# Expert layers of a two-block network: transposes spread over the chunk, sums per eight tiles, gates in 15 steps

## What is computed

```python
def _ffn(x, router_w, router_b, expert_w, expert_b):      # 8 experts, 64 channels
    router_probs = softmax(x @ router_w + router_b)
    top_p, top_i = top_k(router_probs, 2)
    top_p = top_p / sum(top_p)
    expert_out = einsum('bnd,edc->bnec', x, expert_w) + expert_b
    gathered = take_along_axis(expert_out, top_i[..., None], axis=2)
    return einsum('bnk,bnkc->bnc', top_p, gathered)

t = t + _ffn(_ln_t(t), ...)      # _ln_t: layer norm over the 64 channels
```

## Time and profile before

| | |
|---|---|
| median of three runs | 1204.75 us |
| the profiled execution | 1205.99 us, span of its instructions 1204.2 us |
| layer 1, first gate product to last | 276.1 to 585.7 us |
| layer 2, first gate product to last | 888.3 to 1191.6 us |
| busy: PE, DVE, POOL, ACT | 912.3, 911.8, 660.4, 576.0 us |
| granted TensorE clock, mean | 0.886 of 2.4 GHz |

### The profile page before, as it was taken

How to read it: one execution, slowest core, us unless ns; L and a number is a source line. 1 busy time by engine, 2 the same in 40 slices (tenths; PEclk the granted TensorE clock), 3 DMA queues, 4 the chain that set the end, 5 groups by cost and what they waited for, 6 DMA issues and landing times.

```text
span 1204.2 us, 24945 instructions
## 1 busy us (share of the span) xinstructions
PE 912.3 (76%) x8490; PEld 699.6 (58%) x8490; DVE 911.8 (76%) x2088; ACT 576.0 (48%) x1163; POOL 660.4 (55%) x532
## 2 busy tenths in 40 slices
PE   5964469776778777887369999999247887788887
PEld 5863468663445444554269999999124454445454
DVE  6978976677977788799956777754568788777884
ACT  1336854476655565530034444442576556555500
POOL 1542000325877687778474443310437777787787
PEclk9955579977889999999879999999559998899998
DMA  9865600010899992000358778883000000000000
GB/s 387 280 280 118 165 2 1 2 43 0 325 397 398 396 397 90 1 2 1 116 169 281 266 253 277 268 268 118 1 1 18 36 19 35 17 24 29 36 32 39
DMA packets 52865, 168.18 MB, mean 140 GB/s; under 512 B 13616, under 2 KB 13872, under 8 KB 51120
## 3 DMA queue, kind: packets, MB, share of 16 engines
q1 hardware_dynamic: 52784, 167.18, 39.3%
HBM read 98.68 MB, written 68.49 MB: 139 GB/s over the span
## 4 chain that ended last, share of the span: by engine, by line
PE 40%; DVE 24%; ACT 17%; issue 9%; POOL 6%; DMA 2%; ACTq 1%; DVEq 0%; SPq 0%; POOLq 0%
PE pair L1364 19%; ACT pair L1047 10%; DVE R L784 5%; PE pair L1332 5%; PE pair L1282 3%; PE pair L1329 3%; POOL R L458 3%; DVE R L829 3%; DVE work L612 2%; PE pair L1318 2%; PE pair L1319 2%; DVE R L721 2%; PE pair L1296 2%; DVE work L603 2%; ACT X L1081 1%
## 5 line engine op out<-in xcount | busy, mean ns | idle before, releaser
L784 DVE TENSOR_TENSOR R<-pair,R 128x1024 f32<-128x1024 f32 x256 | 310.0, 1215 | 96.7 <-PE pair L1319 90.6
L458 POOL TENSOR_TENSOR R<-R 128x1024 f32<-128x1024 f32 x128 | 304.4, 2378 | 123.1 <-DVE R L784 122.0
L1364 PE MATMUL pair<-R 128*128 (+4 forms) x2880 | 227.8, 243 | 21.6 <-DVE R L836 21.6
L1364 PEld LDWEIGHTS pair<-R 128*128 128x128 f16 x2880 | 224.9, 98 | 24.7 <-issue 22.0
L1318 PE MATMUL pair<-work,R 128*128 128x512 f16 x512 | 203.3, 397 | 35.6 <-DVE R L784 35.5
L1319 PE MATMUL pair<-work,R 128*128 128x512 f16 x512 | 201.2, 393 | 0.0
L1047 ACT ACTIVATE pair<-X,work 128x64 f32 (+1 forms) x496 | 168.8, 394 | 25.2 <-DVE R L721 20.0
L468 POOL TENSOR_TENSOR R<-R 128x512 f32<-128x512 f32 x128 | 163.1, 1274 | 11.3 <-POOL R L458 2.5
L845 DVE COPY R<-R 128x1152 f32<-128x1152 f32 x64 | 91.4, 1429 | 78.9 <-PE pair L1364 78.1
L1329 PE MATMUL pair<-X,ident_sb 128*128 128x256 f32 (+1 forms) x256 | 89.6, 434 | 76.3 <-ACT X L1081 67.0
L1332 PE MATMUL pair<-R,ident_sb 128*128 128x256 f32 x512 | 145.2, 410 | 0.0
(11 more groups left out here) (131 smaller groups left out, 1408.4 us busy)
## 6 DMA issues: line engine op xcount, KB each, us to landing
taps_halves<-R SPq DMA_DIRECT2D x128, 458.5 KB, 6.4
R<-taps_halves SPq DMA_DIRECT2D x64, 917.0 KB, 4.7
R<-spec_re SPq DMA_DIRECT2D x34, 256.0 KB, 4.1
X<-x_rows SPq DMA_DIRECT2D x4, 2048.0 KB, 20.9
R<-x_chan SPq DMA_DIRECT2D x4, 2048.0 KB, 25.3
X<-x_tok SPq DMA_DIRECT2D x4, 2048.0 KB, 13.9
out<-X SPq DMA_DIRECT2D x16, 512.0 KB, 2.6
R<-taps SPq DMA_DIRECT2D x2, 603.0 KB, 7.2
```

What stands on the lines that cost most here:

```text
L458: pool.tensor_tensor(h, pr[:, :, 0:256], pr[:, :, 256:512], ALU.add).then_inc(half_ready, 1)
L784: dve.tensor_tensor(pr.rearrange("p (k c) -> p k c", c=C), pair[p % 2][:, :].rearrange("p (k c) -> p k c", c=C), g.unsqueeze(2).to_broadca ...
L1364: mm = pe.matmul(acc[:, y0:y1, x0:x1, :], blocks[i % 2][:, ks, 2 - y, 1 - x, :], src[:, y0 + y:y1 + y, x0 + x:x1 + x, :], start=(ks == 0 a ...
```

## The change

All of it is in the expert layers.

1. **Sums per eight tiles.** `sum_quad` becomes `sum_octet`: six matmuls in one go, four times a chunk, ahead of pairs 3, 7, 11 and 15 (SUM_AT = 3), for the octet of the four pairs that end four pairs earlier. ACT copies 512 columns instead of 256, at pairs 0, 4, 8, 12. There are eight buffers for POOL's results instead of four.
2. **Transposes spread.** TURN_AT goes from (0, 1, 3, 5) to (9, 13, 1, 5), the first two of them in the chunk before; the routing matmuls follow (ROUTE_AT). `copy_parts` waits for fewer pairs.
3. **Halves of normalisation.** The eight ACTIVATEs are issued as four and four, in two neighbouring pairs, with `copy_parts` between them.
4. **Gates in 15 steps** over pairs 8 to 14. The two small TENSOR_SCALARs (L762, L766) go; ACT computes one of them (`scale_c`), the other is folded away.
5. **One function table.** A set of functions with ln and exp is loaded once at the start.
6. PARTS_AT shifts two of the statistics by a pair.

```diff
-        quarter = [R1[:, 12288 + 512 * i:12288 + 512 * (i + 1)] for i in range(4)]
+        quarter = [R1[:, 512 * i:512 * (i + 1)] for i in (24, 25, 26, 27, 0, 1, 2, 3)]
...
-        GATE_STEPS = 17
+        GATE_STEPS = 15
...
-        NORM_AT, LOW_AT, TURN_AT, ROUTE_AT = (5, 9, 13, 1), (8, 12, 0, 4), (0, 1, 3, 5), (1, 2, 4, 6)
-        NORM_AHEAD, LOW_AHEAD = 3, 2
-        SUM_LAG, COPY_AT = 3, 0
-        GATES_AT = {7: (0, 1), 8: (2, 3), 9: (4, 5), 10: (6, 7), 11: (8, 9), 12: (10,), 13: (11, 12, 13, 14), 14: (15, 16)}
-        PARTS_AT = (0, 1, 1, 2, 3, 3, 5, 6)
+        NORM_AT, LOW_AT, TURN_AT, ROUTE_AT = (5, 9, 13, 1), (8, 12, 0, 4), (9, 13, 1, 5), (0, 1, 3, 7)
+        FIRST_ROUTE = (2, 3, 4, 7)
+        NORM_AHEAD, LOW_AHEAD, TURN_AHEAD = 3, 2, 2
+        SUM_AT, SUM_LAG, COPY_LAG = 3, 1, 2
+        GATES_AT = {8: (0, 1), 9: (2, 3), 10: (4, 5), 11: (6, 7), 12: (8, 9), 13: (10, 11), 14: (12, 13, 14)}
+        PARTS_AT = (1, 2, 2, 3, 3, 5, 6, 7)
...
                 elif i == 11:
-                    dve.wait_ge(exped, n + 1)
-                    ins = dve.tensor_scalar(den, gs[6], SCALE, SCALE, ALU.mult, ALU.add)
+                    ins = dve.scalar_tensor_tensor(out=scratch, in0=scratch, scalar=-5e29, in1=other, op0=ALU.is_le,
+                                                   op1=ALU.subtract)
                 elif i == 12:
+                    dve.wait_ge(exped, 2 * n + 2)
                     ins = dve.reciprocal(first_share, den)
                 elif i == 13:
-                    ins = dve.tensor_scalar(second_share, first_share, -1.0, 1.0 / SCALE, ALU.mult, ALU.add)
-                elif i == 14:
-                    ins = dve.scalar_tensor_tensor(out=e(first), in0=e(scratch), scalar=-5e29, in1=over_e(first_share),
-                                                   op0=ALU.is_le, op1=ALU.mult)
-                elif i == 15:
-                    ins = dve.tensor_tensor(e(logits), e(logits), over_e(second_share), ALU.mult)
+                    ins = dve.tensor_tensor(e(scratch), e(scratch), over_e(first_share), ALU.mult)
                 else:
-                    ins = dve.tensor_tensor(gate[q], logits, first, ALU.add)
+                    ins = dve.scalar_tensor_tensor(out=gate[q], in0=other, scalar=1.0 / SCALE, in1=scratch, op0=ALU.mult,
+                                                   op1=ALU.add)
...
+            act.preload_act_table_set("natural_log_exp_and_others")
...
-                if not isinstance(k, int) or k >= 2:
-                    act.wait_ge(y_ready, (layer * NCHUNK + k - 1) * NPAIR)
-                elif layer:
-                    act.wait_ge(y_ready, layer * NCHUNK * NPAIR)
+                if layer or not isinstance(k, int) or k >= 2:
+                    act.wait_ge(y_ready, (layer * NCHUNK + k - 2) * NPAIR + 4 * (j + 1))
...
+                act.wait_ge(exped, 2 * n + 1)
+                act.activation(gs[3], gs[6], ACT.Identity, bias=scale_c, scale=SCALE).then_inc(exped, 1)
...
-                act.copy(X[:, bass.ds((k * NQUAD + g) * 256, 256)], bank[7][:, 0:256]).then_inc(sum_copied, 1)
+                act.copy(X[:, bass.ds((k * NOCT + o) * 512, 512)], bank[7]).then_inc(sum_copied, 1)
...
-            def sum_quad(layer, k, g):
+            def sum_octet(layer, k, o):
...
+                pe.wait_ge(quarter_ready, 2 * n + 2)
...
+                for i in range(2):
+                    w = quarter[(2 * o + i) % 8].rearrange("p (t j c) -> p t j c", t=4, c=C)
+                    pe.matmul(bank[7][:, 256 * i:256 * (i + 1)], ident_sb[:, :],
+                              X[:, bass.ds((k * NOCT + o) * 512 + 256 * i, 256)], start=True, stop=False)
+                    for j in range(2):
+                        mm = pe.matmul(bank[7][:, 256 * i:256 * (i + 1)], ident_sb[:, :], w[:, :, j, :],
+                                       start=False, stop=(j == 1))
                 mm.then_inc(summed, 1)
...
-                    if p % 2 == 0 and not (isinstance(k, int) and k == 0 and p < 2 * SUM_LAG):
-                        sum_quad(layer, k, p // 2 - SUM_LAG)
+                    if p % 4 == SUM_AT and not (isinstance(k, int) and k == 0 and p < 4 * SUM_LAG):
+                        sum_octet(layer, k, p // 4 - SUM_LAG)
                     expert_pair(layer, k, q, p)
```

More of the change, by code:

```diff
@@ L339, in _ @@
             sp.wait_ge(taps_out, P * 16)
[L340 removed]
+            sp.wait_ge(sum_copied, NOCT * NCHUNK)
             def load_bands(c, i):
@@ L733, in over_e @@
                     return t.unsqueeze(2).to_broadcast([P, CT, NE])
-                best, second, key_max, den, first_share, second_share = gs[0:6]
-                pick, first = gt
+                best, second, key_max, den, first_share = gs[0:5]
+                pick, other = gt
                 rank_b = rank_sb[:, 0:NE].unsqueeze(1).to_broadcast([P, CT, NE])
@@ L1032, in root_seed, with normalise @@
                 act.activation(tok_tmp[6], tok_tmp[5], ACT.Exp, scale=-0.5).then_inc(tok_step, 1)
-            def normalise(layer, k, q, j):
+            def normalise(layer, k, q, j, tiles=range(8)):
                 n = layer * NCHUNK + k
@@ L1038, in normalise @@
                 by_pool = startup and j % 2 == 1
-                if j == 0:
-                    act.wait_ge(tok_step, (n + 1) * TOK_STEPS)
-                if by_pool:
-                    act.wait_ge(tok_normed_p, j + 1)
-                elif layer or j or not (isinstance(k, int) and k == 0):
-                    act.wait_ge(tok_low, n * 4 + (j - 1 if startup and j else j))
-                for t in range(0 if by_pool else 8):
+                if 0 in tiles:
+                    if j == 0:
+                        act.wait_ge(tok_step, (n + 1) * TOK_STEPS)
+                    if by_pool:
+                        act.wait_ge(tok_normed_p, j + 1)
+                    elif layer or j or not (isinstance(k, int) and k == 0):
+                        act.wait_ge(tok_low, n * 4 + (j - 1 if startup and j else j))
+                for t in range(0) if by_pool else tiles:
                     at = 8 * j + t
@@ L1049, in normalise @@
                                           scale=small[2 * q + 1][:, at:at + 1])
+                if 7 not in tiles:
+                    return
                 if not by_pool:
@@ L1097, in expert_chunk @@
                         root_seed(layer, k + 3)
-                    if normed and p in NORM_AT[:NORM_AHEAD]:
-                        normalise(layer, k + 2, q, NORM_AT.index(p))
             def unpack_low(c, i, j):
@@ L1162, in _ @@
                 expert_chunk(layer, 7, 1, False, False, False)
-                for g in range(NQUAD - SUM_LAG, NQUAD):
-                    copy_sum(layer, NCHUNK - 1, g)
+                for o in range(NOCT - COPY_LAG, NOCT):
+                    copy_sum(layer, NCHUNK - 1, o)
                 if layer == 0:
@@ L1339, in expert_chunk @@
                     expert_pair(layer, k, q, p)
-                    if following and p in TURN_AT:
+                    first = isinstance(k, int) and k == 0
+                    if first and p < TURN_AHEAD:
+                        turn_tokens(layer, 1, 1, p)
+                    if following and p in TURN_AT[TURN_AHEAD:]:
                         turn_tokens(layer, k + 1, 1 - q, TURN_AT.index(p))
-                    if following and p in ROUTE_AT:
-                        route(layer, k + 1, 1 - q, ROUTE_AT.index(p))
+                    if normed and p in TURN_AT[:TURN_AHEAD]:
+                        turn_tokens(layer, k + 2, q, TURN_AT.index(p))
@@ L1346, in _ @@
+                    routes = FIRST_ROUTE if first else ROUTE_AT
+                    if following and p in routes:
+                        route(layer, k + 1, 1 - q, routes.index(p))
             offsets = [(0, 0)] + [(y, x) for x in (-1, 0, 1) for y in range(-2, 3) if (y, x) != (0, 0)]
```

72 lines of the change are left out of this document (36 added, 36 removed).

## The result

The changed kernel takes **1191.9 us** (1190.6 to 1194.0) against 1206.0 (1203.9 to 1208.9): a ratio of 0.988, 95% interval 0.985 to 0.991. The forecast was 1215 us, slower. The value lies inside its range of 1186 to 1227, the sign is wrong. The profiled execution has a span of 1188.8 us, 15.4 less than before.

A forecast was written before the change was run, and what follows sets the result against it. No engine bounded the whole; in expert chunks DVE waited for PE, PE for ACT's copy. Terms -14.5 -1.8 +7.3 -1.4 +4.2 +11.8 +4.9 = +10.5 on 1205.99 gave 1216.5, stated as 1215 us after a 1.2 adjustment; range 1186 to 1227.

The forecast's parts named there:

- Table loads: At both expert layers' starts, twelve ACT loads of 1.283 us leave the chain of waits: -14.5 us, bounds -6 and -15.4.
- The ring: Expert chunks: PE's sum waits for POOL's quad, which needs the preceding pairs and gate products; 8.99 us per four pairs.
- the wait for the low half: Looped chunks: PE reaches the transposes before DVE has made the low half of normalisation; adds 1.6 us a chunk.
- 37.6 us a chunk without falls: Looped chunk length at full PE clock: 36.0 us plus 1.6 us of waits at the transposes.
- the ring alone at 36.0: Rival for looped chunks: no waits at transposes and no clock falls, 1170 us; chance 0.05 shared with the covered-sums rival.
- neither at some 33: Rival for looped chunks: sums covered, DVE ends each chunk, some 33 us; total about 1137, chance 0.05 in either form.
- Two falls a chunk at 1.5 us: Looped chunks: PE's clock drops to 1.2 GHz twice after idle gaps, adding 3.0 us, to 40.6; chance 0.47.
- Rival 1: PE's clock holds in the loops and chunk 5: 29 us less, 1186 us; chance 0.17 shared with loads alone.
- Chunks 0: First chunk of both expert layers: no sum before pair 7, -1.8 us for both, ends 0 and -5.
- Gates: Expert chunks: two DVE steps go, 2.1 us a chunk, but DVE does not end a chunk; counted as nothing, bound -31.
- Halves of normalisation: ACT in the expert chunks: 23 us of work less 2.6 in 37 to 41, so no effect on time.
- rival 5: Whole kernel: only the table loads save time, new and old order cost the same, 1190 us; chance 0.17 shared.

The follow-up runs named there:

- the later edits: Changed kernel with sums one turn (four pairs) later, 1169.5 us; with transposes two pairs later, 1178.8 us; with both, 1101.0 us.
- the one-table kernel: Kernel before the change, with only ACT's one function table loaded once at its start: 1184.9 us, ratio 0.983.

## Why the prediction was wrong

- **Table loads, -14.5: right, too small.** 16.2 us at the two starts by putting the line in, 17.8 in all by taking it out.
- **The ring, 8.99 us per four pairs: right as a length** (8.81; 7.51 with half a sum taken out), and it did what was said in chunks 6 and 7: +9.2 in layer 2 for +11.8 forecast. In the looped chunks it was not what PE waited for (0.2 us a chunk). There the wait for the low half was the longer of two bounds.
- **37.6 us a chunk without falls: 0.8 too much** (36.8). I had added the waits for the low half (1.6) to the ring (36.0). The two partly lie on each other: with the ring alone a chunk is 35.6, with the low half's wait alone some 36, with both 36.8, and only without both does it come to 32. Adding was a fair estimate of the length and a poor picture of the cause. Both states that the later edits brought stand among my rivals, the ring alone at 36.0 (35.6 measured) and neither at some 33 (32.2 measured), but I took them for ways in which this change might turn out and not for the next two edits.
- **Two falls a chunk at 1.5 us: the step that failed.** In layer 2's loop the size was right, 1.6 to 1.75 us, and the number was not: two in four chunks, not eight. What the falls cost there is 3.3 us (150.5 less 4 x 36.8) for a forecast of 12: 9 of the 12 us by which this loop was missed, the other 3 being the 0.8 a chunk above. In layer 1's loop, 6 us better than forecast, it is another story. The clock was low for longer than before the change (0.93 of 161.1 us is about 23 us at half clock, 0.96 of 159.7 about 13), but filling the gaps took only 6.7 us out of it, where I had counted 12. Chunks 5 had one fall each for 1.7 and came 4 us better together. Taken together these turn the sign. I read "two falls a chunk" in layer 2's loop before as a property of the kernel's gaps. The same program brings 163.8 or 154.9 us in one loop, and the earlier trace rows held the warning: a chunk of 37.28 at 1.00 beside those of 41. That is half of the story: the new order had two falls in this loop in each of three executions, and no run says why. Rival 1 (the clock holds) comes nearest in layer 2's loop, with 1186 us in all for 1191.9 measured and a chance of 0.17 that was too low; in layer 1's loop the clock did not hold, and there it was wrong.
- **Chunks 0, -1.8: wrong in sign**, +1.2 for both together; no run looks into it.
- **Gates: nothing, right.** Up to 2 us in chunks 5 and 6, nothing in the loops. Halves of normalisation were put at nothing too, and no run tests them alone; nor does one test PARTS_AT, which moves seven of the eight statistics and not two.
- **The shape of the gain.** By the medians the changed order is a loss (+4 to +7 us by the runs with and without the table; only the first is clear of noise), as forecast; I put it at +25, most of the excess in falls. By its number rival 5 (only the table loads count, 1190 us) came nearest, but it had the two parts wrong: the loads gave more, and the order took some of it back.

## What to carry to other kernels

When waits are taken away one at a time and nothing moves, take away two: bounds of nearly equal length hide each other, and here two edits that left a loop at 150 us took 22 us out of it together. A one-line part of a change (here one table load at the start) is to be run alone before the rest gets credit; here it was at least as good as the whole. And before a clock fall is priced per chunk, compare the same chunk in several stretches and executions: if it comes at two lengths, the price belongs in the range, not in the forecast.

## What the runs showed of the chip that I had not expected

- The same gap does not bring the same clock: after 2.28 us of idleness the same eight transposes took 1.04 us at 986.27 and 0.62 at 1024.47. Within one program, executions differ by it: the one-table kernel ran from 1177 to 1191 us, and loops of the same code took 155 or 164 us. The kernels whose gaps were filled spread by 3 and 4 us; the changed kernel itself does no more than that, 3.4.
- A PE that does useless work in its gaps can make a kernel faster: 56 added matmuls a loop took 11 us out of layer 2's loop, 20 out of the whole.
- Removing the gaps did far more than filling them (1182 us), since the waits went with them: with both waits gone, PE's longest gap in a chunk is 0.9 us, the clock is 1.00 in every looped chunk of layer 2, and the kernel takes 1101 us.
